# Last batch of a fused attention and int8 feed-forward kernel: SyncE's gather of the denominators, its large loads, and VectorE's product, each moved in the order of a half

## The reference

```python
q, k, v = LN(x) @ Wq.T, ctx @ Wk.T, ctx @ Wv.T        # per head of 32
e       = exp(clip(q @ k.T / sqrt(32), -50, 50))
x       = x + ((e @ v) / e.sum(-1)) @ Wo.T
n       = LN(x); s = absmax(n, row) / 127
x       = x + (int8(n / s) @ int8(rhs / rs)) * s * rs
```

## Time and profile before

| what | value |
|---|---|
| median of 3 executions | 1805.69 us (1801.85 to 1808.26) |
| the profiled execution, its own time | 1804.89 us |
| its span in the profile | 1803.0 us |
| TensorE busy over the span | 1726.4 us, 96% |
| VectorE busy | 1374.0 us, 76% |
| ScalarE busy | 1313.9 us, 73% |
| DMA queue 1, share of 16 engines | 62.3% |

### The profile page before, as it was taken

How to read it: one execution, slowest core, us unless ns; L and a number is a source line. 1 busy time by engine, 2 the same in 40 slices (tenths; PEclk the granted TensorE clock), 3 DMA queues, 4 the chain that set the end, 5 groups by cost and what they waited for, 6 DMA issues and landing times.

```text
span 1803.0 us, 30538 instructions
## 1 busy us (share of the span) xinstructions
PE 1726.4 (96%) x10808; PEld 1017.6 (56%) x10808; DVE 1374.0 (76%) x1648; ACT 1313.9 (73%) x1729; POOL 118.8 (7%) x76
## 2 busy tenths in 40 slices
PE   7999999999999999999999999999999898988987
PEld 7895655556565565656565565655655343343433
DVE  5657777777778878788886878888786778787776
ACT  4557778778777777778777777877777777776774
POOL 0000000000001010010101001000100101010101
PEclk9999999999999999999999999999999999999998
DMA  7686555556666565666565566755658786768732
GB/s 254 212 244 156 150 142 138 142 145 164 146 161 158 156 164 140 185 157 182 142 159 159 139 189 152 180 147 155 166 128 219 196 202 147 172 147 213 185 95 76
DMA packets 233285, 295.94 MB, mean 164 GB/s; under 512 B 28200, under 2 KB 138792, under 8 KB 232616
## 3 DMA queue, kind: packets, MB, share of 16 engines
q1 hardware_dynamic: 230968, 289.21, 62.3%
q10 hardware_dynamic: 2160, 4.72, 0.9%
HBM read 201.59 MB, written 92.00 MB: 163 GB/s over the span
## 4 chain that ended last, share of the span: by engine, by line
PE 80%; DVE 8%; issue 5%; ACT 4%; DMA 3%; SPq 1%; POOL 0%; POOLq 0%; DVEq 0%; ACTq 0%
PE tile L922 24%; PE wsum L960 22%; PE scores L944 21%; DVE acc L1479 4%; PE tile L992 3%; ACT probs L1192 3%; PE scores L922 2%; PE tile L986 2%; PE scores L1090 1%; DMA den_c<-denoms 1%; PE tile L1053 1%; PE tile L1090 1%; DMA v_parts<-v_stage 1%; PE tile L1030 1%; DVE kmax L499 1%
## 5 line engine op out<-in xcount | busy, mean ns | idle before, releaser
L1192 ACT ACTIVATE probs<-scores 128x1024 f32<-128x1024 f32 x939 | 914.1, 1027 | 229.7 <-PE scores L944 177.2
L1479 DVE TENSOR_TENSOR acc<-acc,probs 128x2048 f32<-128x2048 f32 x384 | 878.6, 2288 | 131.9 <-ACT probs L1192 122.3
L960 PE MATMUL wsum<-probs,v_sb 128*32 128x512 f32 x4096 | 501.1, 608 | 0.0
L944 PE MATMUL scores<-q_stack,k_stack 128*128 128x512 f32 x1536 | 444.4, 410 | 9.7 <-ACT probs L1192 9.1
L944 PEld LDWEIGHTS scores<-q_stack,k_stack 128*128 128x128 f32 x1536 | 265.5, 188 | 223.0 <-ACT probs L1192 111.8
L960 PEld LDWEIGHTS wsum<-probs,v_sb 128*32 128x32 f32 x4096 | 111.6, 110 | 256.4 <-issue 231.1
L1569 POOL TENSOR_TENSOR rstd<-var_eps,minus_half 128x1 f32<-128x1 f32 x48 | 79.6, 1658 | 1259.1 <-DVE var_eps L1378 1259.1
L1090 PE MATMUL scores<-q_stack,k_stack 128*128 128x512 f32 x342 | 110.2, 424 | 21.3 <-ACT probs L1192 21.3
L1430 DVE TENSOR_TENSOR squares<-squares 128x128 bf16<-128x128 bf16 x160 | 35.5, 222 | 124.0 <-ACT squares L1232 123.7
L1479 DVE TENSOR_TENSOR acc<-probs 128x2048 f32<-128x2048 f32 x32 | 73.4, 2292 | 60.8 <-ACT probs L1192 59.7
L922 PE MATMUL tile<-ctx_hi,wk_hi 128*128 128x256 f32 x412 | 116.5, 283 | 1.8 <-DVE ctx_lo L1388 1.8
(11 more groups left out here) (236 smaller groups left out, 2051.9 us busy)
## 6 DMA issues: line engine op xcount, KB each, us to landing
k_stack<-k_parts SPq DMA_DIRECT2D x312, 256.0 KB, 7.4
q_stack<-q_parts SPq DMA_DIRECT2D x124, 256.0 KB, 6.7
v_sb<-v_parts SPq DMA_DIRECT2D x80, 256.0 KB, 6.6
v_parts<-v_stage SPq DMA_DIRECT2D x64, 256.0 KB, 5.0
raw<-ctxT SPq DMA_DIRECT2D x27, 512.0 KB, 7.8
k_parts<-stage_hi SPq DMA_DIRECT2D x96, 128.0 KB, 3.5
k_parts<-stage_lo SPq DMA_DIRECT2D x96, 128.0 KB, 2.0
x_in<-x SPq DMA_DIRECT2D x33, 256.0 KB, 3.7
```

Source lines behind the costliest of these rows:

```text
L944: last = nc.tensor.matmul(scores[:, h, :], k_stack[:, kt // 4, h, (kt % 4) * P:(kt % 4 + 1) * P], q_stack[:, qb, h, :], start=True, stop=True)
L960: last = nc.tensor.matmul(wsum[DH * h:DH * h + DH, :], v_sb[:, kt, DH * h:DH * h + DH], probs[:, n % RING, h, :], start=(kt == 0), stop=(k ...
L1192: nc.scalar.activation(probs[:, slot % RING, 2 * pair:2 * pair + 2, :], score_banks(seg, slot, pair), ACT.Exp, scale=1.0 / math.sqrt(DH)). ...
L1479: nc.vector.tensor_tensor(acc[:, :, :], other, probs[:, slot % RING, :, :], ALU.add).then_inc(sems["add_done"], 1)
```

## The change

In the final segments alone:

- SyncE gathers the denominators at slot first+1 instead of first+2.
- The load of the next half's queries goes from step 1 to step 8, without its wait of its own. The fourth quarter of the keys goes from step 2 to step 5. The first and second quarter for the next half go one step later (5 to 6, 9 to 10); the third stays at 13. The v loads keep their steps.
- The loads of attention rows that stood at slot 16 go to slot 27, but for two of 256 KB in part 2 (`rows_loaded2`).
- The store and load of a row tile that stood at slot 1 stand at slot 3.
- VectorE takes the product straight after the addition of slot first+8, ahead of the row work and of the addition of slot first+9.

```diff
-                    if slot == first + 2:
+                    if slot == first + (1 if seg.final else 2):
                         ct.wait_alone(sp, "denoms_copied", k)
                         sp.dma_start(den_c[:, :], denoms[0:P:DH, :]).then_inc(sems["denoms_spread"], 16)
...
-                    if step == 2:
+                    if step == 3:
                         if i == 0:
                             all_parts_stored(ct, "v_stored")
+                        ct.wait_alone(sp, "step_summed", KT * half)
+                        load_v(j, 3)
+                    if step == 5:
                         ct.wait_alone(sp, "scores_full", 2 * KT * half)
                         load_k(sp, j, 3)
-                    if step == 3:
-                        ct.wait_alone(sp, "step_summed", KT * half)
-                        load_v(j, 3)
                     if i + 1 < 2 * G:
-                        if step == 1:
-                            ct.wait_alone(sp, "scores_full", 2 * KT * half)
+                        if step == 8:
                             load_q(sp, j_next, qb_next, (i + 1) % 2)
                         for quarter in range(3):
-                            if step == 4 * quarter + 5:
+                            if step == 4 * quarter + 6 - (quarter == 2):
...
-                    if slot == 16 and c != 1:
+                    if slot == 16 and c == 2:
                         ct.wait_alone(sp, "o_stored", 0)
-                        if c == 0:
-                            ct.wait_alone(sp, "tile_full", 0)
-                            load_o_rows(sp, 1, slice(0, G), slice(0, QB), "rows_loaded1")
-                        if c == 2:
-                            sp.wait_ge(fs["o_full"], 4)
-                            load_o_rows(sp, 2, slice(0, G), slice(0, P), "rows_loaded2")
-                            load_o_rows(sp, 2, slice(0, G), slice(P, QB), "rows_loaded6")
-                        if c == 3:
-                            sp.wait_ge(fs["o_full"], 8)
-                            load_o_rows(sp, 3, slice(0, 2), slice(0, QB), "rows_loaded3")
+                        sp.wait_ge(fs["o_full"], 4)
+                        load_o_rows(sp, 2, slice(0, G), slice(0, P), "rows_loaded2")
+                    if slot == 27 and c == 0:
+                        ct.wait_alone(sp, "o_stored", 0)
+                        ct.wait_alone(sp, "tile_full", 0)
+                        load_o_rows(sp, 1, slice(0, G), slice(0, QB), "rows_loaded1")
+                    if slot == 27 and c == 2:
+                        load_o_rows(sp, 2, slice(0, G), slice(P, QB), "rows_loaded6")
+                    if slot == 27 and c == 3:
+                        ct.wait_alone(sp, "o_stored", 0)
+                        sp.wait_ge(fs["o_full"], 8)
+                        load_o_rows(sp, 3, slice(0, 2), slice(0, QB), "rows_loaded3")
...
-                    for at, stored, loaded in ((1, -1, 1), (15, 0, 2), (21, 1, 3)):
-                        if slot == at and (c or at > 1):
+                    for at, stored, loaded in ((3, -1, 1), (15, 0, 2), (21, 1, 3)):
+                        if slot == at and (c or at > 3):
...
                         add(even)
+                        product(even)
                         n = row_tile(seg, pair, "norm")
...
                         invert(even)
-                        normalise(even)
+                        low(even)
                     return
```

More of the change, by code:

```diff
@@ L1487, in invert, with product @@
                             nc.vector.reciprocal(recip_c[:, :], den_c[:, :]).then_inc(sems["recips_ready"], 1)
-                def normalise(even):
+                def product(even):
                     for first, k, on in ((0, 0, seg.prev and seg.b), (KT, 1, seg.b)):
@@ L1495, in normalise, with low @@
                             nc.vector.tensor_tensor(sums[:, :], sums[:, :], denoms[:, :], ALU.mult).then_inc(sems["attn_normed"], 1)
+                def low(even):
+                    for first, k, on in ((0, 0, seg.prev and seg.b), (KT, 1, seg.b)):
                         if on and even == first + 12:
```

## The result

The changed kernel takes 1814.56 us (median of 8 executions, 1810.57 to 1816.38), the kernel before 1806.53 in the same runs (8 executions). The ratio is 1.0046, with a 95% interval of 1.0029 to 1.0063: 8 us slower, where 9 us faster was forecast. The span of the profiled execution is 1813.3 us against 1803.0.

A forecast was written before the change was run, and what follows sets the result against it. No engine was taken as full; VectorE's waits for gathered denominators and ScalarE's for the product made halves longer. Gains of 1.8 + 4.5 + 2.8 = 9.1 us took the median from 1805.69 to 1796.6 us, range 1789 to 1803.

The forecast's parts named there:

- The gather in half 0: Half 0: issuing the gather ahead of the query load shortens VectorE's stall, worth 1.8 us, bounds 0 and 1.9.
- Half 5: Half 5: with most loads no longer ahead of the gather, VectorE's stall goes, worth 4.5 us, bounds 4.1 and 4.5.
- Half 1's stall worth nothing: Half 1: removing VectorE's 1.0 us wait for the gather saves nothing.
- The product: Odd halves: the earlier product brings ScalarE's high part 0.70 us forward, 2.8 us over four; even halves gain nothing.
- What the moves cost: SyncE's queue: later loads, the fourth key quarter tightest, still arrive in time; cost 0, at most 1 us per odd half.
- the second rival: Halves 2 and 6: 8 us of transfers spill ahead of the gather, stalling up to 4 us; 1799 to 1803, chance 0.22.
- The slower rival: All eight halves: the fourth key quarter lands late and TensorE, ScalarE and VectorE stand; 1811 us, chance 0.07.
- The clock rival: Odd halves: shorter TensorE gaps also avoid falls to the low clock, 1.1 to 1.6 us each; 1790 to 1792, chance 0.10.

The follow-up runs named there:

- x3: The kernel before with one edit, the gather at slot first+1 in the final segments: 1795.56 us against 1805.47, ratio 0.9947.
- y3: The kernel before with one edit, the row loads of slot 16 at slot 27: 1798.61 us against 1807.98, ratio 0.9947.
- x4: The kernel before with one edit, the product straight after the addition of slot first+8: 1804.69 us against 1805.47, ratio 0.9994.
- y1: The kernel before with two edits, the early gather of x3 and the early product of x4: 1801.86 us against 1807.98, ratio 0.9966.
- y4: The changed kernel with the product back behind the addition of slot first+9: 1810.38 us against 1807.98, ratio 1.0021.
- x2: The changed kernel with separate buffers for high and low part in the final segments, so ScalarE's copy needs no store: 1795.54 us against 1805.47, ratio 0.9943.
- x1: The changed kernel with the row loads of slot 27 at slot 18, behind the gather: 1799.42 us against 1805.47, ratio 0.9964.
- z3: The changed kernel with the row loads back at slot 16 and the product at its old place: 1797.04 us against 1806.62, ratio 0.9946.
- y2: The kernel before with the early gather and slot 16's row loads (but two of 256 KB in part 2) at slot 18: 1795.66 us against 1807.98, ratio 0.9933.
- z1: The kernel before with the early gather and the row loads of slot 16 at slot 27: 1795.15 us against 1806.62, ratio 0.9941.

## Why the prediction was wrong

**The gather in half 0** was sized at 1.8 us; the half got 2.8 us shorter, and 4.2 in x3, where it also has the full clock. The stall left is 1.52 us, near the 1.8 worked out. The bound behind it was taken too tight: the addition after the inversion starts 11.34 us after the first (1396.79 against 1385.45), not 12.23 as in half 2.

**Half 5** was sized at 4.5 us. It got 5.4 shorter, of which 0.9 belongs to the product: right. y3, with the product last and no stall in that half, has it at 46.47 us, 4.5 shorter.

**Half 1's stall worth nothing**: right. y3 has no stall there and the half takes 46.44 us against 46.48. The 2.5 us of the change are 0.9 of the product and 1.6 of the clock, 1.00 instead of 0.96; x4 has 44.09 at 1.00 with the stall still there.

**The product**, 0.70 us in each odd half: 0.86 in half 3, 0.8 in x4. Right in mechanism and size in the odd halves. The even halves were said to stay; at a like clock they mostly got 0.2 us longer, and half 4 lost its full clock (49.62 against 47.78). Alone it shows no gain (x4), and with the early gather, or in the change, the versions with it have ratios that are 0.19 and 0.25 points weaker (y1 against x3, the change against y4). The term of 2.8 us is thus not borne out in the time.

**What the moves cost** is the step that failed. It named the engines that wait for the gather and for the keys, and put 0 to 1 us in each odd half. It did not ask who waits for the other transfer on that queue, the store of the normalised half, although the code has that wait in front of the very copy that starts the chain. The backlog itself was foreseen: the second rival had 8 us of transfers spilling into the next half, and the store came 9.3 us later. But it was priced against the gather, which has 12 us of room there, and not against ScalarE's copy, which came 0.8 us after the first addition of half 2 (1482.33 against 1481.55). So a spill that was thought to cost 0 to 4 us cost 18.1 us in halves 2 and 6, the clock's share included. x2 takes the wait away and x1 the backlog, and they return 1.0% and 0.8% of the time; y4 shows that the stalls do not come from the product. The 0.07 that the forecast gave to a slower kernel stood for late keys alone; this cause was not among the rivals.

**The slower rival** (late keys) did not happen, though the time went the way it said: TensorE shows no wait for `k_stack` in the final segments, and z3 is faster than the kernel before. The clock rival is answered only in part: with 1.90 us of waiting for the exponentials instead of 2.78 half 1 kept its clock, halves 3 and 5 with 1.90 and 1.91 did not.

## What to carry to other kernels

When loads are moved later in an in-order queue, list every transfer that will stand behind them, stores too, and for each the engine that waits for it, the earliest moment it does, and its slack. A store that frees a reused buffer is on the path of the engine that refills the buffer. And try the smallest edit first: here one moved line had the whole gain, and late row loads (y3) and late keys and queries (z3) were each nearly harmless until both stood ahead of the store.

## What the runs showed of the hardware

ScalarE's stall in half 2 cost more than its length, and TensorE came back from it at 1.2 GHz: 9.2 us of delay (the copy could have gone when TensorE's sum ended, near 1478.6) made the half 10.6 us longer.

The clock's spells go with the order of work in a way I cannot explain. Of halves 2, 4 and 6 in the profiled executions, none of 21 is at 1.00 in the seven kernels with the product first, and 9 of 21 are in the seven with it last (the kernel before, x3, y2, y3, y4, z1, z3). At full clock such a half mostly takes 47.8 us, at 0.97 49.4 with the product last. This may be what cancels the product's gain. The halves are those of one execution of each kernel; over the whole span, the clock is 0.987 to 0.990 in all 12 executions of y1 and 0.990 to 0.993 in all 6 of x3, which has the product last, but they ran on different chips and y1 has the wait for the inverses besides. No run here separates it.
